# A four-layer graph kernel: Pool forms the fourth head's weights in every second unit of the last layer's later chunks, with a re-ordered end and earlier shifts in layer 0

## The chip, the cores and the metric

The kernel runs on one core of one Trainium2 chip. The metric is device time in microseconds (us), the median of several executions. The core's engines run side by side, each from its own queue of instructions, and wait for each other through semaphores: PE (TensorE, matrix products into the eight PSUM banks), DVE (VectorE), ACT (ScalarE), Pool (GpSimd) and SP, which only issues transfers here.

## The reference

The input is x (2708 nodes x 256 features) and a sparse matrix adj (2708 x 2708, non-negative, diagonal set). Four graph layers follow each other, each as x = layernorm(x + layer(x, adj)). Cut to the two that the change touches:

```python
# layer 0: three attention heads (and two GRU cells, left out here)
att = jnp.where(edge_adj > 0, e_plus[None, :], NEG_INF)
att = jax.nn.softmax(att, axis=1)
edge_support += att * edge_adj @ hW            # per head; adj without its diagonal
...
# layer 3: four heads of 64 features
h = (x @ W).reshape(n, HEADS, C)
e = leaky_relu(s_src[:, None, :] + s_dst[None, :, :], 0.2)
e = jnp.where((adj > 0.5)[:, :, None], e, -1e9)
alpha = softmax(e, axis=0)
out = jnp.einsum('ijh,ihc->jhc', alpha, h).reshape(n, 256) + bias
```

## The kernel before

The nodes are cut into T = 22 tiles of 128 rows; the last has 20. A sweep computes a result for all 2708 target columns, chunk by chunk; for each chunk it goes over the 22 source tiles. One tile in one chunk is a *unit*, and n = c x 22 + t numbers the units of a sweep. All loops over units are written out on every engine; the order of the code is the order in each engine's queue.

**The last layer (layer 3)** has CW = 3 chunks of 1,024, 1,024 and 660 columns, 66 units. The softmax's exponential is factored, so that a head's weight is a maximum of two known factors times the mask:

- SP loads a strip of adj (`strip3`, three buffers).
- ACT makes the mask from it in two passes (`above`, `masked`; L1493, L1500), bf16, three buffers. `masked(n)` waits until DVE has used unit n-3's mask.
- DVE forms the weights, one `scalar_tensor_tensor` a head, four a unit (L2116): PM3 = max(r3, s) x mask, f32, as wide as the chunk, three buffers. Unit n waits until PE is done with unit n-3.
- PE multiplies: features of heads 0 and 1 into banks 0 and 1, of heads 2 and 3 into banks 2 and 3 (L1164), and the sums of the weights, the degrees, into banks 4 and 5 (L1177), in matmuls that fill a quarter of the array's columns each. A unit of 1,024 columns is 32 + 16 recorded matmuls.

At a chunk's end ACT copies the six banks into rawT3 (`chunk_out`, three copies, L1508), when all matmuls of the chunk are done; PE opens each accumulator of the next chunk (L897) when its copy is there. The chunk's eight tiles of output are finished in pairs among the units of the next chunk (`pair_at`): PE turns a pair back (`backs`, six transposes, L1148), DVE makes the divisors (`divisors`, L2071 to L2077), Pool adds a term for rows without an edge (two tensor_tensor of 256 columns a tile, L833 and L835), ACT scales the eight head pieces (`scaled`, L1517), DVE adds (`added`, L2084) and takes statistics, ACT the root (L1524), DVE normalizes (`normed`, L2102), SP stores. The last chunk's three pairs (`LAST`) come one after another at the end. In layer 2 Pool has adds of 256 columns (L813) beside DVE weights of 496 (L2043).

**Layer 0's weighted sweep** has six chunks of 4, 4, 4, 3, 3 and 4 tiles (512, 512, 512, 384, 384 and 404 columns) and 132 units. Per unit: ACT `distances` (two relu passes, L1315), DVE `clamped` (L1752), ACT `exponentials` (L1322), DVE `weighted` (L1770), PE 12 recorded matmuls (L1051; 4 in the last unit, L1054). The weights E have three buffers; `distances(n)` and `clamped(n)` wait for PE to end unit n-3. The softmax's denominators of the later tiles come from work that goes on between the units: for each row tile a bias (L1677) and three heads, each one long custom DVE operation of 2708 columns (L1687), its negation (L1698) and a long ACT exponential (L1286). `ROWS_AT` says at which units these stand. When a chunk's rows are ready, its shifts are made: ACT a logarithm (`denominators`, L1292, with a table load before and one after it), DVE `shifts`, PE `maxima_turned`, ACT `maxima_out`, and SP stores a row (m_rows), waits for the store and spreads it to all partitions (m_bc), all in `maxima_row` at t = 20 of the chunk before. The first unit of the chunk waits for it.

Of the kernel before, what the change touches and what calls it, by code (L numbers as in the profile page):

```python
# [22 lines left out]
R = P  # L23
# [129 lines left out]
class WideLoad:  # L153


    def __init__(self, i):
# [17 lines left out]
SHIFTS_AT = 16  # L174
assert all(ROWS_AT[i][H0] < (chunk_of(i) - 1) * T + SHIFTS_AT for i in ROWS_AT)
# [4 lines left out]
def build(nc, x, adj, gat_W, gat_a, e_Wih, e_Whh, e_bih, e_bhh, n_Wih, n_Whh, n_bih, n_bhh,  # L180
# [15 lines left out]
    with ExitStack() as ctx:  # L196
# [99 lines left out]
        E = sb(3, H0, W)  # L296
        units_end = top[0]
# [119 lines left out]
        ln1_x = sem("ln1_x")  # L417
# [54 lines left out]
        LAST = range((CW - 1) * DT // 2, T // 2)  # L472

# [125 lines left out]
        def maxima_row(sp, c):  # L599
# [3 lines left out]
            load(sp, m_rows[c:c + 1, 0:H0 * nt * R].rearrange("a (k p) -> (a k) p", p=R), rows_s[0:H0 * nt, 0:R], m_out)  # L603
            sp.wait_ge(m_out, 16 * c)
# [36 lines left out]
        def _(sp):  # L641
# [58 lines left out]
            for n in range(3, UNITS):  # L700
# [4 lines left out]
                if c + 1 < CH and t == 20:  # L705
                    maxima_row(sp, c + 1)
# [29 lines left out]
            sp.wait_ge(ln2_x, T)  # L736
# [35 lines left out]
        def _(pool):  # L772
# [55 lines left out]
            for v in range(T // 2):  # L828
                pool.wait_ge(fin_zz, v + 1)
# [6 lines left out]
                pool.sem_inc(fin_zero, 1)  # L836


        def pe_project(pe, i, wcat, cols, between=None):
# [60 lines left out]
        def _(pe):  # L900
# [137 lines left out]
            for n in range(UNITS):  # L1038
# [9 lines left out]
                for h in range(H0 if t < T - 1 else 1):  # L1048
                    for f in range(KD):
                        if t < T - 1:  # L1050
                            ins = PE.matmul(bank(2 * (c % 2) + f)[:, 0:wid(c)], hs[0:R, m % 3, h * D + f * P:h * D + (f + 1) * P],  # L1051
                                            E[0:R, n % 3, h, 0:wid(c)], start=t == 0 and h == 0, stop=False)
                        else:
                            ins = PE.matmul(bank(2 * (c % 2) + f)[:, 0:wid(c)], hs_tail[0:STACK, f * P:(f + 1) * P],  # L1054
                                            E[0:STACK, n % 3, 0, 0:wid(c)], start=False, stop=True)
                ins.then_inc(s["mm_done"], 1)
                if t == 17 and c + 1 < CH:
                    maxima_turned(c + 1)
# [91 lines left out]
            for n in range(UNITS3):  # L1150
                c, t = divmod(n, T)
                halves = [(v, min(BANK, wide(c) - v * BANK)) for v in range(-(-wide(c) // BANK))]
                for h in range(0, H3, 2):
                    if t == 0:
                        if c:
                            pe.wait_ge(l3_read, RAW3 * (c - 1) + h // 2 + 1)
                        for v, w in halves:
                            opened(h + v)
                    if c == 0:
                        pe.wait_ge(l3_scaled, t + 1)  # L1160
                    pe.wait_ge(l3_p, n * H3 + h + 2)
                    for v, w in halves:
                        for q in range(P // DQ):
                            PE.matmul(bank(h + v)[q * DQ:(q + 1) * DQ, 0:w], proj3[0:kp(t), t, h * C3 + q * DQ:h * C3 + (q + 1) * DQ],  # L1164
                                      PM3[0:kp(t), n % 3, h + q * DQ // C3, v * BANK:v * BANK + w], start=False, stop=t == T - 1,
                                      skip_group_check=True)
                if t == 0:
# [5 lines left out]
                    for v, w in halves:  # L1173
                        opened(4 + v)
# [10 lines left out]
            for v in LAST:  # L1185
                backs(v)
# [966 lines left out]
```

## Time and profile before

| | |
|---|---|
| median of three runs | 2177.42 us (2175.49 to 2177.68) |
| the profiled execution | 2175.57 us |
| its span, first to last instruction | 2173.9 us |
| mean granted clock of PE | 0.977 of full |
| last layer's sweep, PE's first to last matmul | 1814.7 to 2150.5 |
| behind it, to the end of the span | 23.3 us |

The profile is one execution. Busy shares are shares of the span; matmuls are pipelined and their ends modelled, so that neighbouring ones overlap in the records, as DVE's do by under 0.1 us.

### The profile page before, as it was taken

The page shows a single profiled execution, that of the slowest core. Times are in us where ns is not written, and L with a number is a line of the kernel's source. Part 1 is how long each engine was busy: PE and PEld are TensorE (multiplying, and loading weights), DVE is VectorE, ACT ScalarE, POOL GpSimd, SP SyncE. Part 2 cuts the span into 40 slices and gives each one's busy share as a digit, 9 for nine tenths or more (in the row PEclk, how much of TensorE's full clock was granted, in tenths as well). Part 3 has the DMA queues.
Part 4 walks back from the last instruction along what each step waited for, and adds up shares of the span by engine and source line. Part 5 has one row for each costly group of instructions (what it writes and reads, how often), then busy time and mean ns, then how long its engine had stood idle before and what let it go on. Part 6 is the DMA issues. An engine that isn't in the chain of part 4 may idle for free.

```text
span 2173.9 us, 28504 instructions
## 1 busy us (share of the span) xinstructions
PE 2064.6 (95%) x10803; PEld 1159.6 (53%) x10803; DVE 1549.1 (71%) x2621; ACT 963.2 (44%) x1505; POOL 132.2 (6%) x169
## 2 busy tenths in 40 slices
PE   7999999899999999999999999999999978999996
PEld 4556665344444455555555534557999953333242
DVE  4665557797978875443778853444899956989997
ACT  3222226798888877664222210002121246644442
POOL 0000000000000000000001010000010040002011
PEclk9999999899999999999999999999999989999997
DMA  7665645455555554742000034541100115332231
GB/s 232 217 213 190 202 141 201 172 205 189 177 180 194 198 165 160 230 139 95 0 1 0 0 103 127 132 130 45 51 23 20 39 41 187 103 94 87 80 89 34
DMA packets 133176, 265.69 MB, mean 122 GB/s; under 512 B 15258, under 2 KB 62904, under 8 KB 130200
## 3 DMA queue, kind: packets, MB, share of 16 engines
q1 hardware_dynamic: 114712, 234.50, 34.0%
q10 hardware_dynamic: 18324, 29.34, 3.6%
q8 instruction: 86, 1.41, 0.3%
q14 instruction: 54, 0.44, 0.1%
HBM read 220.43 MB, written 43.36 MB: 121 GB/s over the span
## 4 chain that ended last, share of the span: by engine, by line
PE 64%; DVE 23%; ACT 8%; issue 4%; DMA 1%; POOL 0%; DVEq 0%; SPq 0%; ACTq 0%; POOLq 0%
PE banks L1051 20%; PE banks L954 9%; PE banks L1102 9%; PE banks L1136 6%; DVE arena L2116 5%; PE banks L1164 5%; PE banks L943 3%; DVE arena L2043 3%; PE banks L1177 3%; ACT arena L1286 2%; PE banks L995 2%; PE banks L861 2%; DVE arena L1687 2%; DVE arena L1770 1%; DVE arena L1871 1%
## 5 line engine op out<-in xcount | busy, mean ns | idle before, releaser
L1051 PE MATMUL banks<-arena 128*128 128x512 f32 (+2 forms) x1512 | 588.4, 548 | 19.4 <-DVE arena L1770 19.2
L1051 PEld LDWEIGHTS banks<-arena 128*128 128x128 f32 x1512 | 285.4, 191 | 312.2 <-issue 234.8
L1770 DVE TENSOR_TENSOR arena<-arena 128x1536 f32<-128x1536 f32 (+4 forms) x132 | 201.6, 1527 | 157.8 <-ACT arena L1322 150.4
L2116 DVE SCALAR_TENSOR_TENSOR arena<-arena 128x1024 f32<-128x1024 f32 (+3 forms) x264 | 293.1, 1181 | 16.0 <-PE banks L1177 13.2
L1164 PE MATMUL banks<-arena 128*32 128x512 f32 (+3 forms) x2112 | 221.3, 555 | 13.5 <-DVE arena L2116 13.5
L954 PE MATMUL banks<-arena 128*128 128x512 f32 (+4 forms) x528 | 222.5, 543 | 0.2 <-ACT arena L1227 0.2
L1136 PE MATMUL banks<-arena 128*124 128x129 f32 (+2 forms) x1936 | 217.7, 274 | 4.0 <-DVE arena L2043 3.3
L1136 PEld LDWEIGHTS banks<-arena 128*124 128x124 f32 (+2 forms) x1936 | 214.6, 186 | 7.3 <-DVE arena L2043 4.8
L1102 PE MATMUL banks<-arena 128*128 128x512 f32 (+4 forms) x528 | 207.7, 547 | 5.1 <-DVE arena L1872 3.7
L1315 ACT ACTIVATE arena<-arena 128x512 f32<-128x512 f32 (+4 forms) x264 | 162.8, 662 | 82.7 <-PE banks L1051 76.5
L1687 DVE CUSTOM_DVE_ANT_0 arena<-arena 128x2708 f32<-128x2708 bf16 (+1 forms) x66 | 196.2, 2973 | 1.6 <-DMA arena<-e_rows 1.3
L1322 ACT ACTIVATE arena<-arena 128x1536 f32<-128x1536 f32 (+4 forms) x132 | 170.7, 1294 | 40.1 <-DVE arena L1752 39.4
L2043 DVE SCALAR_TENSOR_TENSOR arena<-arena 128x496 f32<-128x496 f32 (+2 forms) x264 | 171.9, 709 | 21.1 <-PE banks L1136 14.4
L1286 ACT ACTIVATE arena<-arena 128x2708 f32<-128x2708 f32 (+1 forms) x66 | 168.0, 2546 | 11.7 <-DVE arena L1698 11.7
L1227 ACT COPY arena<-banks 128x512 f32<-128x512 f32 (+4 forms) x132 | 70.8, 536 | 210.3 <-PE banks L943 209.9
L1102 PEld LDWEIGHTS banks<-arena 128*128 128x128 f32 (+1 forms) x528 | 98.8, 190 | 105.1 <-issue 73.9
L1164 PEld LDWEIGHTS banks<-arena 128*32 128x32 f32 (+1 forms) x2112 | 70.9, 111 | 148.9 <-issue 128.6
L1635 DVE TENSOR_SCALAR arena<-arena 128x512 bf16<-128x512 f32 (+4 forms) x132 | 52.2, 395 | 112.9 <-ACT arena L1227 112.6
L1858 DVE TENSOR_SCALAR arena<-arena 128x512 uint8<-128x512 f32 (+4 forms) x132 | 51.9, 399 | 97.0 <-DMA arena<-adj_T 96.7
L954 PEld LDWEIGHTS banks<-arena 128*128 128x128 f32 (+1 forms) x528 | 89.6, 190 | 51.6 <-issue 36.1
L1177 PE MATMUL banks<-arena 128*32 128x512 f32 (+3 forms) x1056 | 114.6, 548 | 0.0
L1500 ACT ACTIVATE arena<-arena 128x1024 bf16<-128x1024 f32 (+1 forms) x66 | 69.1, 1047 | 65.5 <-DVE arena L2116 65.4
(224 smaller groups left out, 2236.4 us busy)
## 6 DMA issues: line engine op xcount, KB each, us to landing
arena<-hw_rows SPq DMA_DIRECT2D x126, 384.0 KB, 3.1
arena<-adj_T SPq DMA_DIRECT2D x126, 256.0 KB, 3.2
arena<-in_adj SPq DMA_DIRECT2D x17, 1354.0 KB
arena<-in_adj SPq DMA_DIRECT2D x42, 512.0 KB
adj_T<-arena ACTq DMA_DIRECT2D x63, 256.0 KB, 2.3
arena<-adj_T SPq DMA_DIRECT2D x84, 192.0 KB, 3.0
arena<-in_adj SPq DMA_DIRECT2D x15, 1024.0 KB
arena<-in_adj SPq DMA_DIRECT2D x15, 768.0 KB
```

Source lines behind the costliest of these rows:

```text
L954: PE.matmul(bank(2 * (c % 2) + f)[:, 0:w], xnat[0:k, t, f * P:(f + 1) * P], AT[0:k, n % 4, 0:w], start=t == 0, stop=t == T - 1)
L1051: ins = PE.matmul(bank(2 * (c % 2) + f)[:, 0:wid(c)], hs[0:R, m % 3, h * D + f * P:h * D + (f + 1) * P], E[0:R, n % 3, h, 0:wid(c)], start ...
L1102: ins = PE.matmul(bank(2 * (c % 2) + f)[:, 0:wid(c)], xd[0:kp(t), t, f * P:(f + 1) * P], strips1[0:kp(t), n % 4, 0:wid(c)], start=t == 0, ...
L1136: ins = PE.matmul(bank(b0 + k // 3)[0:nr, (k % 3) * (C2 + 1):(k % 3 + 1) * (C2 + 1)], PM2[0:kp(t), n % 3, h, r * R2:r * R2 + nr], proj2[0: ...
L1164: PE.matmul(bank(h + v)[q * DQ:(q + 1) * DQ, 0:w], proj3[0:kp(t), t, h * C3 + q * DQ:h * C3 + (q + 1) * DQ], PM3[0:kp(t), n % 3, h + q * D ...
L1177: ins = PE.matmul(bank(4 + v)[h * DQ:(h + 1) * DQ, 0:w], g3[0:kp(t), t, h, :], PM3[0:kp(t), n % 3, h, v * BANK:v * BANK + w], start=False, ...
L1286: S.activation(srow[0:kp(i), j % 2, :], srow[0:kp(i), j % 2, :], ACT.Exp, bias=negm[0:kp(i), h, i:i + 1], accum_out=den[0:kp(i), h, i:i + ...
L1322: S.activation(e, e, ACT.Exp, scale=-1.0).then_inc(s["y_ok"], 1)
L1687: link(V.tensor_tensor_reduce(out=srow[0:nr, sl, :], in0=bias[0:nr, :], in1=e_bc[0:nr, h, :], scale=1.0, scalar=3 * NEG, op0=ALU.add, op1= ...
L1770: V.tensor_tensor(e, e, a, ALU.mult).then_inc(s["p_ok"], 1)
L2043: V.scalar_tensor_tensor(PM2[0:k, n % 3, h, 0:w], r2_bc[0:k, h, c * CW2:c * CW2 + w], smalls[0:k, 4, h * T + t:h * T + t + 1], mask2[0:k, ...
L2116: V.scalar_tensor_tensor(PM3[0:k, n % 3, h, 0:w], r3_bc[0:k, h, c * WW:c * WW + w], smalls[0:k, 4, h * T + t:h * T + t + 1], mask3[0:k, n ...
```

## The change

Three things are changed together.

1. In the last layer, for every odd t of the second and third chunk but the very last unit (`by_pool`, 21 units), Pool forms head 3's weights in two instructions, a tensor_scalar (maximum) and a tensor_tensor (times the mask), with a semaphore of its own, l3_q; DVE forms three heads there. `weights_there` waits on both. Pool's terms for rows without an edge (`zero_terms`) are queued between these.
2. The last layer's end: `chunk_out` copies the banks of features as soon as their last matmul is done (l3_out). In the last unit PE does the degrees first, then the features of heads 0 and 1, the degrees' six transposes, the features of heads 2 and 3, and twelve transposes. DVE makes all divisors at once, and scales and adds in one instruction a head and tile, straight from PSUM; ACT's scalings and two of Pool's three rounds fall away there (their terms come to DVE).
3. In layer 0, the shifts of the chunks after the first two are made 2 to 10 units earlier (`SHIFTS_AT`), the store and the spread of the maxima stand a unit apart in SP's queue, rows 18 to 21 have other places (`ROWS_AT`), and the two chunks of 384 columns use the buffer of the weights as four parts (`E_narrow`, `weights_of`, `weights_free`). Two semaphores (ln1_x, ln2_x) become one.

```diff
-           14: (46, 47, 48, 49), 15: (50, 51, 52, 54), 16: (55, 56, 57, 58), 17: (59, 60, 61, 62), 18: (64, 65, 66, 67),
-           19: (69, 70, 72, 74), 20: (76, 77, 79, 81), 21: (83, 84, 86, 88)}
+           14: (46, 47, 48, 49), 15: (50, 51, 52, 54), 16: (55, 56, 57, 58), 17: (59, 60, 61, 62), 18: (64, 65, 67, 69),
+           19: (71, 72, 74, 76), 20: (78, 79, 81, 83), 21: (85, 86, 88, 90)}
...
-SHIFTS_AT = 16
+SHIFTS_AT = {0: 16, 1: 14 + T, 2: 12 + 2 * T, 3: 12 + 3 * T, 4: 6 + 4 * T}
+SHIFTS = {n: c + 1 for c, n in SHIFTS_AT.items()}
...
+        def by_pool(n):
+            return n >= T and n % T % 2 == 1 and n < UNITS3 - 1
...
+        def weights_there(eng, n, h):
+
+            eng.wait_ge(l3_p, vector_weights(n) + min(h + 1, H3 - by_pool(n)))
+            if h == H3 - 1 and pool_weights(n + 1):
+                eng.wait_ge(l3_q, pool_weights(n + 1))
...
+        def weights_of(n):
+            if n in NARROW:
+                return E_narrow[:, (n - NARROW[0]) % 4]
+            return E[:, (n if n < NARROW[0] else n - NARROW[-1] - 1) % 3]
+
+        def weights_free(eng, n):
+            if n >= 3:
+                eng.wait_ge(sw["C"]["mm_done"], n - 3 if n in NARROW[3:] else n - 2)
...
-                if c + 1 < CH and t == 20:
-                    maxima_row(sp, c + 1)
+                if n - 4 in SHIFTS:
+                    maxima_stored(sp, SHIFTS[n - 4])
+                if n - 5 in SHIFTS:
+                    maxima_spread(sp, SHIFTS[n - 5])
...
+            pool.wait_ge(rest_bc["r3"], 16)
+            for n in range(T, UNITS3):
+                c, t = divmod(n, T)
+                if by_pool(n):
+                    k, w = kp(t), wide(c)
+                    pool.wait_ge(l3_mm, n - 2)
+                    pool.wait_ge(l3_mask, n + 1)
+                    p = PM3[0:k, n % 3, H3 - 1, 0:w]
+                    link(G.tensor_scalar(p, r3_bc[0:k, H3 - 1, c * WW:c * WW + w],
+                                         smalls[0:k, 4, (H3 - 1) * T + t:(H3 - 1) * T + t + 1], None, ALU.max))
+                    G.tensor_tensor(p, p, mask3[0:k, n % 3, 0:w], ALU.mult).then_inc(l3_q, 1)
+                if pair_at(n, 5) is not None:
+                    zero_terms(pair_at(n, 5))
+            zero_terms(LAST[-1])
...
+            degrees(UNITS3 - 1).then_inc(l3_mm, 1)
+            features(UNITS3 - 1, 0)
+            pe.wait_ge(fin_scaled, LAST[0])
+            pe.wait_ge(l3_read, RAW3 * (CW - 1) + 1)
+            for i, g in enumerate(LAST_TILES):
+                ins = PE.transpose(bank(6, 2)[:, i * P:(i + 1) * P], rawT3[:, 2, g % DT * R:(g % DT + 1) * R], ident)
+            ins.then_inc(tail_ps, 1)
+            features(UNITS3 - 1, 2)
+            for k in range(RAW3 - 1):
+                pe.wait_ge(l3_read, RAW3 * (CW - 1) + k + 2)
+                for g in LAST_TILES:
+                    ins = PE.transpose(turned_back(g)[:, k * P:(k + 1) * P], rawT3[:, k, g % DT * R:(g % DT + 1) * R], ident)
+                    if k and g % 2:
+                        ins.then_inc(tail_ps, 1)
...
             def chunk_out(c):
-                act.wait_ge(l3_mm, (c + 1) * T)
                 if c:
                     act.wait_ge(back_ps, c * DT // 2)
-                for k in range(RAW3):
+                for k in (0, 1, 2) if c < CW - 1 else (2, 0, 1):
+                    if k < 2:
+                        act.wait_ge(l3_out, 2 * c + k + 1)
+                    else:
+                        act.wait_ge(l3_mm, (c + 1) * T)
                     S.copy(rawT3[:, k, 0:wide(c)], bank(2 * k, 2)[:, 0:wide(c)]).then_inc(l3_read, 1)
...
-                if c + 1 < CH and t == SHIFTS_AT + 1:
-                    shifts(c + 1)
+                if n - 1 in SHIFTS:
+                    shifts(SHIFTS[n - 1])
...
+            def last_terms(v, terms, factor):
+                for g in (2 * v, 2 * v + 1):
+                    nr = kp(g)
+                    for h in range(H3):
+                        f = slice(h * C3, (h + 1) * C3)
+                        x = xnat[0:nr, g, f]
+                        ins = V.scalar_tensor_tensor(x, terms(g)[0:nr, f], factor[0:nr, g, h:h + 1], x, ALU.mult, ALU.add)
+                link(ins)
...
-                for h in range(H3):
+                for h in range(H3 - by_pool(n)):
                     if n == 0:
                         dve.wait_ge(r3_first[h], 16)
...
-            divisors(LAST[0])
+            last_divisors()
+            for v in LAST[:-1]:
+                last_terms(v, lambda g: sum_bc, zz3)
             for v in LAST:
-                added(v)
-                if v + 1 in LAST:
-                    divisors(v + 1)
-                normed(v)
+                last_added(v)
+                if v > LAST[0]:
+                    normed(v - 1)
+            normed(LAST[-1])
```

## Rows read from the trace of the kernel before

**Rows 1.** The page's table of engines: busy us (share of the span), instructions.
```profile
PE 2064.6 (95%) x10803; PEld 1159.6 (53%) x10803; DVE 1549.1 (71%) x2621; ACT 963.2 (44%) x1505; POOL 132.2 (6%) x169
```

**Rows 2.** Timeline of PE, last layer: start us, us, engine, line, operation, tiles, count.
```profile
1884.83 3.66 PE L1164 MATMUL banks<-arena 128*32 128x512 f32 x32
1889.99 3.67 PE L1164 MATMUL banks<-arena 128*32 128x512 f32 x32
...
2084.32 2.40 PE L1164 MATMUL banks<-arena 128*32 128x512 f32 x32
2087.66 2.40 PE L1164 MATMUL banks<-arena 128*32 128x512 f32 x32
...
2091.91 1.32 PE L1164 MATMUL banks<-arena 128*32 128x512 f32 x16
```

**Rows 3.** Timeline of DVE, second chunk's units 3 and 4; in brackets idle time and its releaser.
```profile
1942.77 4.87 DVE L2116 SCALAR_TENSOR_TENSOR arena<-arena 128x1024 f32<-128x1024 f32 x4 [5.64 <-PE banks L1177]
1947.93 4.88 DVE L2116 SCALAR_TENSOR_TENSOR arena<-arena 128x1024 f32<-128x1024 f32 x4 [0.29 <-PE banks L1177]
```

**Rows 4.** DVE's groups by shape, 1959.8 to 2053.5 and 2066.9 to 2147.8: busy, mean ns, idle.
```profile
L2116 DVE SCALAR_TENSOR_TENSOR arena<-arena 128x1024 f32<-128x1024 f32 x60 | 76.3, 1341 | 0.0
...
L2116 DVE SCALAR_TENSOR_TENSOR arena<-arena 128x660 f32<-128x660 f32 x72 | 63.4, 950 | 2.8 <-PE banks L1177 2.8
```

**Rows 5.** PE's groups, 1942.6 to 2052.4 and 2066.7 to 2147.0: busy, mean ns, idle.
```profile
L1164 PE MATMUL banks<-arena 128*32 128x512 f32 x644 | 73.6, 593 | 2.0 <-DVE arena L2116 2.0
...
L1164 PE MATMUL banks<-arena 128*32 128x512 f32 (+1 forms) x643 | 51.0, 450 | 6.0 <-DVE arena L2116 6.0
```

**Rows 6.** Timelines of Pool and of DVE, the first pair's turn in the second chunk.
```profile
1959.64 0.62 POOL L833 TENSOR_TENSOR arena<-arena 128x256 f32<-128x256 f32 x1 [160.99 <-DVE arena L2074]
1960.34 1.50 POOL L835 TENSOR_TENSOR arena<-arena 128x256 f32<-128x256 f32 x1
1961.92 1.48 POOL L833 TENSOR_TENSOR arena<-arena 128x256 f32<-128x256 f32 x1
...
1961.26 4.79 DVE L2116 SCALAR_TENSOR_TENSOR arena<-arena 128x1024 f32<-128x1024 f32 x3
```

**Rows 7.** Timelines of DVE and of Pool in layer 2, the same microseconds.
```profile
1619.56 4.10 DVE L2043 SCALAR_TENSOR_TENSOR arena<-arena 128x496 f32<-128x496 f32 x4 [0.38 <-PE banks L1136]
...
1619.72 3.40 POOL L813 TENSOR_TENSOR arena<-arena 128x256 f32<-128x256 f32 x3
```

**Rows 8.** Pool's groups by shape, 0 to 25 us (two rows) and 1790 to 2150.
```profile
L769 POOL TENSOR_TENSOR arena<-arena 128x128 f32<-128x128 f32 x4 | 1.5, 414 | 14.3 <-DMA arena<-in_adj 14.3
L783 POOL MEMSET arena<- 128x704 f32 x1 | 0.7, 691 | 0.0
...
L822 POOL TENSOR_TENSOR arena<-arena 128x256 f32<-128x256 f32 x1 | 0.7, 727 | 0.4 <-PE banks L851 0.4
```

**Rows 9.** Chunk boundaries: a stretch (busy us, granted clock), PE's timeline, DVE's timeline.
```profile
1926.30:1933.30 7.00, 5.90 (x49) 1.36 (x48) 5.92 (x5) 1.05 (x2) 0.00 (x0) 0.83 0.00 0
...
1933.32 1.04 PE L897 MATMUL banks<-arena 128*128 128x512 bf16 x2 [1.12 <-ACT arena L1508]
...
2066.93 5.88 DVE L2116 SCALAR_TENSOR_TENSOR arena<-arena 128x660 f32<-128x660 f32 x7 [2.78 <-PE banks L1177]
```

**Rows 10.** The end: stretch with PE, PEld, DVE, ACT, Pool busy, then a DVE group.
```profile
2150.60:2173.90 23.30, 4.45 (x18) 3.02 (x18) 10.35 (x44) 7.50 (x30) 7.52 (x12) 0.55 0.09 30
...
L2084 DVE TENSOR_TENSOR arena<-arena 128x512 f32<-128x512 f32 (+2 forms) x4 | 2.1, 548 | 2.5 <-POOLq L836 2.5
```

**Rows 11.** Layer 0: stretch of the fourth chunk, chain that ended last, timelines of PE, ACT.
```profile
744.90:842.40 97.50, 87.19 (x259) 47.85 (x257) 69.69 (x78) 78.64 (x93) 6.83 (x3) 0.98 0.51 171
...
772.02 2.91 DVE arena L1687 x2
...
780.63 2.90 DVE arena L1687 x2
...
821.22 5.80 PE L1051 MATMUL banks<-arena 128*128 128x384 f32 x12 [2.75 <-DVE arena L1770]
...
625.74 1.34 ACT L1315 ACTIVATE arena<-arena 128x512 f32<-128x512 f32 x2 [1.63 <-DMA arena<-m_rows]
```

More of the change, by code:

```diff
@@ L173 @@
 LOAD_AT = {ROWS_AT[i][H0] + 1: i + 1 for i in range(RPC, T - 1)}
-SHIFTS_AT = 16
-assert all(ROWS_AT[i][H0] < (chunk_of(i) - 1) * T + SHIFTS_AT for i in ROWS_AT)
+SHIFTS_AT = {0: 16, 1: 14 + T, 2: 12 + 2 * T, 3: 12 + 3 * T, 4: 6 + 4 * T}
+assert all(ROWS_AT[i][H0] < SHIFTS_AT[chunk_of(i) - 1] for i in ROWS_AT)
+SHIFTS = {n: c + 1 for c, n in SHIFTS_AT.items()}
+NARROW = range(sum(s == RPC for s in SIZES[:CH - 1]) * T, (CH - 1) * T)
+assert all((SIZES[c] == RPC) == (c * T not in NARROW) for c in range(CH))
 ROWS_END = ROWS_AT[T - 1][H0]
@@ L827, in _, with zero_terms @@
             pool.wait_ge(sum_ok, 2)
-            for v in range(T // 2):
-                pool.wait_ge(fin_zz, v + 1)
+            def zero_terms(v):
+                pool.wait_ge(fin_zz, min(v, LAST[0]) + 1)
                 for nr, ts in pair_parts(v):
@@ L1149, in backs, with halves, features, degrees @@
                 ins.then_inc(back_ps, 1)
-            for n in range(UNITS3):
+            def halves(c):
+                return [(v, min(BANK, wide(c) - v * BANK)) for v in range(-(-wide(c) // BANK))]
+            def features(n, h):
                 c, t = divmod(n, T)
[L1152 to L1166, printed above, removed]
+                if t == 0:
+                    if c:
+                        pe.wait_ge(l3_read, RAW3 * (c - 1) + h // 2 + 1)
+                    for v, w in halves(c):
+                        opened(h + v)
+                if c == 0:
+                    pe.wait_ge(l3_scaled, t + 1)
+                weights_there(pe, n, h + 1)
+                for v, w in halves(c):
+                    for q in range(P // DQ):
+                        ins = PE.matmul(bank(h + v)[q * DQ:(q + 1) * DQ, 0:w], proj3[0:kp(t), t, h * C3 + q * DQ:h * C3 + (q + 1) * DQ],
+                                        PM3[0:kp(t), n % 3, h + q * DQ // C3, v * BANK:v * BANK + w], start=False, stop=t == T - 1,
+                                        skip_group_check=True)
+                if t == T - 1:
+                    ins.then_inc(l3_out, 1)
+            def degrees(n):
+                c, t = divmod(n, T)
                 if t == 0:
@@ L1178, in _ @@
                                         PM3[0:kp(t), n % 3, h, v * BANK:v * BANK + w], start=False, stop=t == T - 1, skip_group_check=True)
-                ins.then_inc(l3_mm, 1)
+                return ins
+            for n in range(UNITS3 - 1):
+                c, t = divmod(n, T)
+                features(n, 0)
+                features(n, 2)
+                degrees(n).then_inc(l3_mm, 1)
                 v = pair_at(n, 3)
@@ L1305, in distances @@
                     shifts_there(act, c)
-                if n >= 3 and not general:
-                    act.wait_ge(s["mm_done"], n - 2)
+                if not general:
+                    weights_free(act, n)
                 if n < 3:
```

88 lines of the change are left out of this document (55 added, 33 removed).

## The prediction

> **What bounds the kernel now.** I read the page first: Pool is busy 6% of the span [rows 1], which invites moving work to it. But the shares are means over stages, so I took the last layer by stretches. In its first chunk TensorE (PE) paces: its units start 5.16 us apart (1884.83, 1889.99), in the third chunk 3.34 us apart when fed (2084.32, 2087.66), and 0.91 more where a pair is turned back between them (2091.91) [rows 2]. DVE needs 4 x 1.20 = 4.79 us for a unit of 1,024 columns (four instructions in 4.88, less the 0.09 by which neighbours overlap) and waits 0.29 us before each [rows 3]. From the second chunk on DVE also finishes one pair of output tiles every four units, so that its 19 units from 1942.77 to 2053.5 take 110.7 us, 5.8 each, against PE's 5.16 + 0.91/4 = 5.4. DVE is then never idle: zero idle before the 60 weight instructions of 1959.8 to 2053.5 and 2.8 us before the 72 of the third chunk [rows 4]. Yet PE stands still little: 2.0 us of the second chunk's 110 and 6.0 of the third's 80 as separate gaps [rows 5]. By unit starts, 20 units at 5.16 and four turn-backs make 106.9 of 109.8, and 20 at 3.34 with four make 70.5 of 80.3. So a DVE that cost nothing would give 2.9 + 9.8 = 12.7 us at most.
>
> **The Pool part: what it takes from DVE.** By_pool is true for 11 units of the second chunk and 10 of the third. Each takes one weight instruction from DVE: 1.20 us at 1,024 columns, and (0.90 - 0.08) = 0.82 at 660.
>
> **What it gives back.** Pool gets two instructions per such unit, a tensor_scalar and a tensor_tensor as wide as the one removed. The trace shows what Pool and this very DVE instruction do to each other. Pool's 256-wide tensor_tensor takes 0.62 us alone and 1.48 to 1.50 beside DVE weights [rows 6]: it waits for the running one. DVE in turn makes three weights in 4.79 us instead of 2 x 1.20 + 1.28 = 3.68, though Pool did only one operation for each [rows 6]. One 256-wide Pool operation thus costs DVE some 0.38 us. In layer 2, beside three Pool adds, four 496-wide instructions take 4.10 [rows 7]; alone they would take 4 x 0.65 + 0.08 = 2.68 (0.65 from 0.82 at 660, less 164 columns at 1.04 ns, the slope between 1,024 and 660): 0.47 for an add. They take turns, they don't overlap. Being served in turn, DVE loses Pool's own time less about 0.25 (0.62 - 0.38).
>
> The Trainium skill says it of the chip ("SBUF — State Buffer", Who interferes with whom): a DVE instruction with two SBUF inputs and a GpSimd instruction that reads SBUF lock each other out for the whole instruction. By that rule DVE would lose the full 0.62, not 0.38; the sum below would be 9 us larger. The row decides for 0.38. The rule speaks against this change as a whole, and the trace agrees with that.
>
> Sizes. Tensor_tensor at 1,024: four times the 256-wide loss is 1.5 as the lower end; going on with the slope from 0.41 (128 wide) to 0.73 (256 wide) gives 2.6 alone, so 2.4 lost [rows 8]. I take 2.0, between them. The trace has no Pool tensor_scalar. It can't be quicker than a memset, which reads nothing: 0.69 at 704 [rows 8], so 1.0 at 1,024, 0.7 lost; nor slower than the two-input form, 2.0 lost. I take 1.1, near the memset since it has one input stream. Together 3.1 lost (2.2 to 4.4) against 1.2 saved: DVE is worse by 1.9 (1.0 to 3.2) per unit. At 660 the same lines give 1.95 (1.4 to 2.6) against 0.82: worse by 1.13 (0.6 to 1.8).
>
> **Where it lands.** Walk DVE from its last long wait, 1942.77 [rows 3], 1.1 us earlier because the gap before it goes (below). Unit 3: 3.6 + 3.1, unit 4: 4.8, unit 5: 6.7, divisors 0.8: 1960.7, where the profile has 1959.8, the start of the stretch in rows 4; +0.9. From there it has no slack: eight Pool units (7 to 21), 8 x 1.9 = 15.2, so +16.1. Third chunk: unit 1 adds 1.1, the wait of 2.78 before unit 3 [rows 9] is used up, leaving +14.4; nine more, 9 x 1.13 = 10.2: **+24.6 us** when DVE ends its last weight. Low ends: +10.8; high ends: +44. Pool isn't itself late: per four units it has two weights of about 6 us with their turns and four 256-wide operations of 1.5, 18 of 28 us. PE has to wait for whichever of the two ends last, and its slack in the second chunk is only 0.6 per unit. Pool runs ahead because the mask and the buffer of unit n are there once unit n-3 is done. The extra wait on PE's and ACT's queues costs nothing unless Pool is last.
>
> **Chunk boundary.** PE idles 1.12 us before the accumulators are opened, for ACT's copies [rows 9]. They now start when the first features of the last unit are done, about 4 us earlier, ahead of the gap: 1.1 gained at the first boundary (in the walk). At the second DVE sets the time, so nothing.
>
> **The tail.** From DVE's last weight (2147.8) to the end is 26.1 us, 23.3 of it behind PE's last matmul; in these DVE works 10.35 and the rest is waiting in turn on PE, on ACT's scalings and on Pool [rows 10]. Now, from the same point: degree sums and first features 1.1 each (a third of 3.34), six transposes 1.3 (0.91 in the flow), four small DVE steps 0.9: 4.4. Then 16 terms of 64 columns at 0.20 (0.82 at 660, less 596 columns at 1.04 ns) 3.2, and the last pair's four Pool operations beside them, 4 x 0.38 = 1.5: 9.1. The second features, ACT's two copies and twelve transposes hide there (without that cover they end at about 7.6, so nothing shows yet). Then 24 terms, 4.8; what is left of DVE's 10.35 without the additions (2.1, [rows 10]) and the three rounds of divisors (some 2.2), 6.1; hand-overs 0.8; store and end as now 2.3. Sum 23.1: **-3.0** (-1 to -6). What goes from the path is ACT's 24 scalings and Pool's turns; what comes on it is DVE's 40 small terms.
>
> **Layer 0.** Its fourth chunk (384 columns) isn't PE-bound: 97.5 us with PE busy 87.2 [rows 11]. The chain goes round DVE and ACT: row head 2.91, its negation, row exponential, unit exponential, weights, clamp, and the next head 8.61 us later (772.02, 780.63), for two units [rows 11]; PE would need 82.7 for the chunk if each of 21 units took 5.16 x 384/512 = 3.87. A fourth buffer doesn't shorten that ring: it frees waits on PE, and the first three narrow units keep the old one. I give it 0 to 1. The new places of the rows take one head of ten out of this chunk (about 1.5 us) and the logarithm, with two table loads, from right behind a row exponential: its stall of 2.75 before 821.22 [rows 11] halves. With the start of the chunk (rows' heads no longer on three units running) I get 4.0 (2 to 6). Earlier shifts also take away ACT's wait of 1.63 for the m_rows load at the second boundary [rows 11], of which a row exponential behind it hides most: 1.0 (0 to 2). Together **-5.0** (-2 to -8). The store and the spread of the maxima are now two steps of SP's queue, with one unit's loads between them; those are issued sooner than now. Loads ahead stay four deep.
>
> **Sum.** 24.6 - 3.0 - 5.0 = +16.6 on the profiled execution's 2175.57: 2192.2. The median of the runs is 1.85 us above that execution: 2194; I say 2193.
>
> **The rivals.**
> - *No turns to speak of* (Pool's two-step form interferes little, or Pool gets in where DVE waits). Then PE paces: 12.7 + 1.1 + 3.0 + 5.0 = 21.8 less: about 2155. Pool's and DVE's times beside each other speak against it [rows 6]. With x lost per weight at 1,024 (0.63 x at 660) the whole sum is about 14.3 x - 28.6: even at 2.0, faster by more than 0.2% under 1.7.
> - *Only the tensor_tensor interferes* (one input stream passes beside DVE). Loss 2.0 and 1.3: 8 x 0.8 + 0.5 - 2.8 + 9 x 0.48 = +8.4, less 8.0: 2178, no change. Nothing in the trace speaks to it directly.
> - *The clock goes too.* PE will now stand still 1 to 3 us in many units. Today the granted clock falls to the lower of its two levels (1.2 for 2.4 GHz) for part of 1926.3 to 1933.3, 0.83 on average, round the 1.12 us gap [rows 9]; the 12 matmuls behind the 2.75 us gap take 5.80 instead of 4.1 [rows 11]. At the lower level PE needs 10.3 us a unit and would itself pace. With this, or Pool prices at the high ends: about 2212.
>
> **How the numbers follow.** Turns as worked out 0.57, its own range 2178 to 2212; the clock or the high prices 0.13; one stream only 0.16; no turns 0.12; something else 0.02. What a measurement can tell from no change is 0.2%, 4.4 us. Faster: no turns, and a third of one stream: 0.18. Same: half of one stream and the low edge of the first case: 0.13. Slower: 0.69. Range 2170 to 2212, leaving out the no-turns case and half of the clock case.
>
> **What would show it.** DVE's weights beside Pool's: two operations of Pool each, 1.2 to 1.5 us longer than alone, and some DVE weight instructions of 2 to 3.5 us start to start. If these stay at 1.20, the whole forecast falls. The last layer's second chunk about 14 to 18 us longer, the third about 8 longer, PE with gaps before most odd units; first boundary without a gap; from DVE's last weight to the end 23; layer 0's fourth chunk 93 instead of 97.5. The prediction goes wrong first by Pool's tensor_scalar price, which is taken from a memset.

## The result, and the profile after

Before: 2177.18 us, after: 2181.91 us (medians of 16 runs each, 2172.72 to 2181.32 and 2179.48 to 2185.94); ratio 1.002, interval 1.0013 to 1.0028. The change makes the kernel slower by 4.7 us; 16 had been forecast. The profiled execution took 2180.24 us, span 2178.4, clock 0.981.

The page's engines, against [rows 1]:

```profile
PE 2064.0 (95%) x10803; PEld 1151.5 (53%) x10803; DVE 1568.8 (72%) x2625; ACT 957.4 (44%) x1481; POOL 222.3 (10%) x203
```

DVE has 21 weight instructions fewer and is busy 19.7 us longer; 5.6 of that lie in the new end (below), nearly all the rest in the weights' chunks. The groups of DVE and PE in the same stretches as [rows 4, 5] (second chunk 1954.0 to 2056.4 for DVE and 1942.6 to 2062.2 for PE, third 2070.4 to 2156.3 and 2070 to 2155.5), then Pool's from 1910 to 2156:

```profile
L2223 DVE SCALAR_TENSOR_TENSOR arena<-arena 128x1024 f32<-128x1024 f32 x53 | 83.4, 1639 | 0.0
L2173 DVE TENSOR_SCALAR arena<-arena 128x2 f32<-128x2 f32 x4 | 3.3, 827 | 0.1
...
L2223 DVE SCALAR_TENSOR_TENSOR arena<-arena 128x660 f32<-128x660 f32 x63 | 65.5, 1106 | 2.8 <-PE banks L1239 2.8
...
L1220 PE MATMUL banks<-arena 128*32 128x512 f32 x600 | 70.1, 595 | 10.1 <-DVE arena L2223 9.7
...
L1220 PE MATMUL banks<-arena 128*32 128x512 f32 x320 | 42.1, 598 | 11.5 <-DVE arena L2223 11.5
...
L886 POOL TENSOR_SCALAR arena<-arena 128x1024 f32<-128x1024 f32 x10 | 36.1, 3611 | 149.0 <-PE banks L1239 147.9 <-POOL arena L875 1.1
L886 POOL TENSOR_SCALAR arena<-arena 128x660 f32<-128x660 f32 x10 | 24.2, 2424 | 25.9 <-PE banks L1239 24.8 <-POOL arena L875 1.1
L888 POOL TENSOR_TENSOR arena<-arena 128x1024 f32<-128x1024 f32 x10 | 22.5, 2253 | 0.8
```

A DVE weight lasts 1639 ns in the mean for 1341 [rows 4], so seven instructions fewer (53 for 60) cost 7 us more. PE's idle time for DVE has grown from 2.0 to 9.7 and from 6.0 to 11.5 us. Pool waits for buffers that PE has to free and for its own work ahead, and PE never waits for Pool: Pool ended each weight 1.8 us or more before PE's features of heads 2 and 3 started.

How one weight of Pool costs DVE: Pool's timeline, then DVE's, read from three starts, each row covering two neighbouring instructions:

```profile
2035.06 3.53 POOL L886 TENSOR_SCALAR arena<-arena 128x1024 f32<-128x1024 f32 x1 [0.27 <-POOL arena L875]
2038.67 2.32 POOL L888 TENSOR_TENSOR arena<-arena 128x1024 f32<-128x1024 f32 x1
...
2034.22 3.71 DVE L2223 SCALAR_TENSOR_TENSOR arena<-arena 128x1024 f32<-128x1024 f32 x2
2035.80 3.33 DVE L2223 SCALAR_TENSOR_TENSOR arena<-arena 128x1024 f32<-128x1024 f32 x2
2037.85 4.21 DVE L2223 SCALAR_TENSOR_TENSOR arena<-arena 128x1024 f32<-128x1024 f32 x2
```

The weight that starts at 2035.80 ends at 2034.22 + 3.71 = 2037.93, and the next starts at 2037.85: 2.06 us from start to start instead of 1.20, so Pool's tensor_scalar costs 0.86, though it lasts 3.53 itself; the weight at 2037.85 inside that span takes its normal 1.28 (2035.80 + 3.33 = 2039.13). The one behind it ends at 2037.85 + 4.21 = 2042.06 after 3.02 us: the tensor_tensor costs 1.74. At 660 columns the same reading gives 0.55 and 1.10.

Not every weight meets DVE so. Pool's tensor_tensor of unit t = 17, with a DVE instruction of two elements a row out of the statistics of a finished pair, and the DVE instruction of the same kind in e9 (an experiment below), where Pool's tensor_scalar ran beside it:

```profile
2020.37 1.99 POOL L888 TENSOR_TENSOR arena<-arena 128x1024 f32<-128x1024 f32 x1
...
2021.35 1.04 DVE L2173 TENSOR_SCALAR arena<-arena 128x2 f32<-128x2 f32 x1
```

```profile
2009.41 4.26 POOL L886 TENSOR_SCALAR arena<-arena 128x1024 f32<-128x1024 f32 x1 [7.31 <-PE banks L1239]
...
2012.06 0.17 DVE L2173 TENSOR_SCALAR arena<-arena 128x2 f32<-128x2 f32 x1
2012.14 1.28 DVE L2223 SCALAR_TENSOR_TENSOR arena<-arena 128x1024 f32<-128x1024 f32 x1
```

In the first, the tensor_tensor costs DVE 0.87 (1.04 for 0.17) instead of 1.74; in the second the tensor_scalar costs nothing. In the kernel after, t = 13, 17 and 21 of the second chunk are such units.

The end, against [rows 10]: a stretch with the columns given there, then DVE's timeline.

```profile
2157.60:2178.43 20.83, 6.50 (x54) 3.83 (x46) 15.93 (x69) 2.74 (x6) 2.62 (x4) 0.56 0.14 46
```

```profile
2159.63 0.18 DVE L2180 COPY arena<-banks 128x24 f32<-128x24 f32 x1 [2.48 <-PE banks L1257]
...
2160.62 4.51 DVE L2193 SCALAR_TENSOR_TENSOR arena<-arena 128x64 f32<-128x64 f32 x16
2165.16 1.63 DVE L2193 SCALAR_TENSOR_TENSOR arena<-banks,arena 128x64 f32<-128x64 f32 x8
```

DVE is now the busy engine there (15.93 of 20.8 us, before 10.35 of 23.3), and from its last weight (2156.30) to the end it is 22.1 us instead of 26.0.

**Where the difference sits.** The last layer cut at six points that every trace has: PE's first matmul of the layer (1), DVE's start of unit 6 in the second chunk (2), its end of unit 21 (3), its start of unit 3 in the third chunk (4), the end of its last weight (5), the end of the span (6). In us:

| kernel | 1-2 | 2-3 | 3-4 | 4-5 | 5-6 |
|---|---|---|---|---|---|
| before | 145.2 | 93.7 | 13.4 | 80.9 | 26.0 |
| after | 144.8 | 102.2 | 14.0 | 85.9 | 22.1 |
| e1: merged parts, no Pool weights | 144.3 | 93.7 | 11.2 | 80.9 | 22.1 |
| e2: Pool part alone | 145.7 | 102.2 | 14.7 | 85.9 | 26.2 |
| e3: layer 0 part alone | 145.3 | 93.7 | 13.4 | 80.9 | 27.0 |
| e4: end part alone | 144.6 | 93.7 | 11.2 | 80.9 | 22.2 |
| e5: Pool writes constants | 144.2 | 85.4 | 18.4 | 75.2 | 22.1 |
| e6: tensor_scalar alone | 144.2 | 89.8 | 14.1 | 77.9 | 22.1 |
| e7: tensor_tensor alone | 144.6 | 94.5 | 14.1 | 80.4 | 22.1 |
| e8: second chunk alone | 145.0 | 102.2 | 12.4 | 80.9 | 22.1 |
| e9: t = 1, 5, 9, ... | 144.0 | 96.5 | 17.4 | 82.3 | 22.1 |
| e10: t = 3, 7, 11, ... | 144.4 | 99.2 | 12.9 | 84.2 | 22.1 |

(Two more executions with the old end, e3 and e11, have 27.0 in 5-6, so the old end itself varies by 1 us.)

After against before: -0.4, +8.5, +0.6, +5.0 and -3.9, with the layer's start 5.25 us earlier (1814.67, 1809.42): +4.6, the difference of the spans being 4.5.

### The profile page after: what moved, and what is told of

Its sections match the earlier page's. It is cut to its first block, busy times and chain, and to the rows that moved or that the text cites. A ratio compares the mean times of both kernels' runs of the same rounds, so it can differ in the third digit from the quotient of the medians.

```text
span 2178.4 us, 28619 instructions
## 1 busy us (share of the span) xinstructions
PE 2064.0 (95%) x10803; PEld 1151.5 (53%) x10803; DVE 1568.8 (72%) x2625; ACT 957.4 (44%) x1481; POOL 222.3 (10%) x203
## 4 chain that ended last, share of the span: by engine, by line
PE 64%; DVE 24%; ACT 6%; issue 3%; DMA 1%; SPq 0%; DVEq 0%; POOL 0%; ACTq 0%; POOLq 0%
PE banks L1106 20%; PE banks L1009 9%; PE banks L1157 9%; PE banks L1191 6%; DVE arena L2223 6%; PE banks L1220 5%; PE banks L998 3%; DVE arena L2120 3%; PE banks L1239 3%; PE banks L1050 2%; DVE arena L1766 2%; ACT arena L1365 2%; PE banks L916 2%; DVE arena L1948 1%; DVE arena L1847 1%
## 5 line engine op out<-in xcount | busy, mean ns | idle before, releaser
L2223 DVE SCALAR_TENSOR_TENSOR arena<-arena 128x1024 f32<-128x1024 f32 (+3 forms) x243 | 301.1, 1309 | 15.5 <-PE banks L1239 12.7
L1220 PEld LDWEIGHTS banks<-arena 128*32 128x32 f32 (+1 forms) x2112 | 65.7, 111 | 171.0 <-issue 125.1
```

What stands on the lines that cost most here:

```text
L1220: ins = PE.matmul(bank(h + v)[q * DQ:(q + 1) * DQ, 0:w], proj3[0:kp(t), t, h * C3 + q * DQ:h * C3 + (q + 1) * DQ], PM3[0:kp(t), n % 3, h + ...
L2223: V.scalar_tensor_tensor(PM3[0:k, n % 3, h, 0:w], r3_bc[0:k, h, c * WW:c * WW + w], smalls[0:k, 4, h * T + t:h * T + t + 1], mask3[0:k, n ...
```

## The experiments

Ratios are to the kernel before, run on the same chip beside each.

**Which part costs what: e1 to e4.** e1 is the kernel after with `by_pool` always false.

```diff
-            return n >= T and n % T % 2 == 1 and n < UNITS3 - 1
+            return False
```

e2 is the kernel before with `by_pool`, its waits and Pool's loop alone; e3 the kernel before with the layer 0 edits alone; e4 the kernel before with the new `chunk_out` and the new end of the last layer alone. Where an expectation speaks of 17 weights, these are the ones inside stretches 2-3 and 4-5; each of these kernels moves all 21.

> The two merged parts alone, with every weight of the last layer on VectorE. Theory A (the merged parts gain what the comparison of the traces shows, about 5.2 us before the last layer and 4.0 us behind its last weight; the Pool part alone loses): 9 us under the kernel before, about 2168 us, VectorE's last weight near 2142.6 us. Theory B (the gains and the loss depend on each other: with the last layer starting 5 us earlier, or without Pool's work, VectorE waits for something else): less than half of that, about 2173 us or more.

> The Pool part alone on the kernel before. Theory A (17 weights by Pool cost VectorE a net 8.5 us in the second chunk and 5.0 us in the third): 13 to 14 us slower, about 2191 us, with the same prices per pair of instructions: beside Pool's tensor_scalar one 1,024-wide weight of VectorE takes 2.06 us from start to start, beside its tensor_tensor 2.9 us. Theory B (part of the loss comes from how the merged parts shift the tail or the opening against Pool): 8 us or less. The prediction on record would have 24.6 us here.

> The first layer's part alone. Theory A: what the sweep of layer 0 wins, about 5.2 us at the last layer's first matmul, arrives at the end in full, since the last layer's order is unchanged: about 2172 us. Theory B (a later layer's clock halving or a wait gives it back): 2174 to 2177 us.

> The part on the last layer's end alone (chunks' ends, divisors, outputs). Theory A: the stretch from VectorE's last weight to the end falls from 26.1 to about 22.1 us and nothing else changes: about 2173 us. Theory B (the shorter end in the comparison came from Pool's or VectorE's load in the last units and not from this part): within 1 us of the kernel before.

| run | median us | ratio (interval) | difference |
|---|---|---|---|
| e1 | 2165.97 | 0.995 (0.9938 to 0.9963) | -11.0 |
| e2 | 2192.84 | 1.0071 (1.0058 to 1.0084) | +15.9 |
| e3 | 2169.84 | 0.997 (0.9959 to 0.9981) | -7.1 |
| e4 | 2170.49 | 0.9967 (0.9954 to 0.998) | -6.5 |

Theory A holds in kind: the parts add up. The Pool part costs 15.9 us on the kernel before, and 4.7 + 11.0 = 15.7 on top of e1. The merged parts win more than I read from two traces (11.0, not 9), and separately 13.6; their intervals (e1 8.1 to 13.5, e3 4.1 to 8.9, e4 4.4 to 10.0) allow both.

e4's 6.5 is seen in the table: 0.6 at the first boundary, 2.2 at the second, 3.9 at the end. "Nothing else changes", as theory A had it, is wrong by the 2.2. Two things make them up. PE's gap of 1.12 us ahead of the accumulators is there at the second boundary of before as well, and e4 has none. And PE's clock is at its lower level for less time. The stretch 2055 to 2070 (the granted clock is the third figure from the right), before, e4, after:

```profile
2055.00:2070.00 15.00, 13.88 (x130) 4.04 (x126) 12.22 (x16) 8.21 (x10) 0.00 (x0) 0.77 0.39 109
2055.00:2070.00 15.00, 15.00 (x134) 4.04 (x130) 14.37 (x19) 8.68 (x11) 0.00 (x0) 0.89 0.42 109
2055.00:2070.00 15.00, 15.00 (x114) 3.49 (x110) 12.81 (x16) 8.92 (x11) 3.85 (x2) 0.77 0.38 106
```

A clock of 0.77 over 15 us is some 6.9 us at half speed, 0.89 some 3.3; the difference is worth about 1.8 us to a busy PE. In before the gap lies within the spell, so the two don't add up in full. e1 and e8 have 0.89 round this boundary too, e2 0.77. So in the kernel after the Pool part takes the 2.2 back: by the delay of PE described under e8, and by the longer spell. That the new `chunk_out` or Pool's work sets the spell's length isn't shown.

**What Pool's instructions do to DVE: e5 to e7.** Each is the kernel after with another body for Pool's weight. e5 leaves the maximum and the mask of these weights out, e6 the mask, e7 the maximum.

```diff
 # e5
-link(G.tensor_scalar(p, r3_bc[...], smalls[...], None, ALU.max))
-G.tensor_tensor(p, p, mask3[0:k, n % 3, 0:w], ALU.mult).then_inc(l3_q, 1)
+link(G.memset(p, 1.0))
+G.memset(p, 1.0).then_inc(l3_q, 1)
 # e6
+G.tensor_scalar(p, r3_bc[...], smalls[...], None, ALU.max).then_inc(l3_q, 1)
 # e7
+G.tensor_tensor(p, r3_bc[...], mask3[0:k, n % 3, 0:w], ALU.mult).then_inc(l3_q, 1)
```

> The kernel after, but Pool writes the constant 1.0 twice where it would form a weight (the maximum and the mask of those 17 weights are left out). It tells the work taken off VectorE from what Pool's reads do to it. Theory A (VectorE is lengthened by instructions of Pool that read SBUF, and keeps its own time beside a write of a constant): VectorE's 1,024-wide weights stay at 1.20 us, 17 of them are gone, TensorE paces the units and the kernel ends near 2156 us. Theory B (any instruction of Pool takes turns with VectorE): a memset of 1,024 lasts 0.69 us alone, so VectorE loses up to 1.4 us a weight, and the time is 2168 us or more, no better than without Pool's work.

> The kernel after with Pool's tensor_scalar alone; the multiplication by the mask is left out for those 17 weights. Theory A (each such instruction costs VectorE 0.86 us at 1,024 and 0.55 us at 660 against 1.20 and 0.82 us saved): VectorE comes out ahead by 0.3 us a weight, so 4 to 5 us faster than with no weight on Pool, about 2163 us. Theory B (the tensor_scalar with a scalar from memory is what costs, and the tensor_tensor rides along): slower than without Pool's work, 2172 us or more.

> The kernel after with Pool's tensor_tensor alone (rows of r times the mask; the maximum is left out for those 17 weights). Theory A (1.74 us lost at 1,024 and 1.10 us at 660 against 1.20 and 0.82 us saved, less what falls beside VectorE's waits): 3 to 7 us slower than without Pool's work, about 2173 us. Theory B (the second read operand makes no difference; two instructions of one kind cost the same): like the kernel with the tensor_scalar alone, within 1.5 us of it.

| run | median us | ratio (interval) | difference | stretches 2 to 5, against e1 |
|---|---|---|---|---|
| e5 | 2159.8 | 0.9919 (0.9899 to 0.9938) | -17.8 | -6.9 |
| e6 | 2160.37 | 0.9923 (0.9902 to 0.9944) | -17.3 | -4.0 |
| e7 | 2169.33 | 0.9962 (0.995 to 0.9975) | -8.3 | +3.2 |

e1 has -11.0, so e5 and e6 are 6.8 and 6.3 us under it and e7 2.7 above. e7's profiled execution is the fastest of its ten (2161.32, its last layer starts at 1803.9), so its stretches are compared and not its span. Pool's and DVE's timelines, first of e5, then of e6, then of e7:

```profile
2018.67 0.95 POOL L886 MEMSET arena<- 128x1024 f32 x1 [8.35 <-PE banks L1238]
2019.68 0.95 POOL L887 MEMSET arena<- 128x1024 f32 x1
...
2015.98 7.27 DVE L2222 SCALAR_TENSOR_TENSOR arena<-arena 128x1024 f32<-128x1024 f32 x6
```

```profile
2013.24 2.84 POOL L886 TENSOR_SCALAR arena<-arena 128x1024 f32<-128x1024 f32 x1 [5.54 <-PE banks L1238]
...
2013.53 0.84 DVE L2172 TENSOR_SCALAR arena<-arena 128x2 f32<-128x2 f32 x1
2014.28 6.06 DVE L2222 SCALAR_TENSOR_TENSOR arena<-arena 128x1024 f32<-128x1024 f32 x5
```

```profile
1999.86 2.70 POOL L886 TENSOR_TENSOR arena<-arena 128x1024 f32<-128x1024 f32 x1 [0.24 <-POOL arena L875]
...
1997.42 11.01 DVE L2221 SCALAR_TENSOR_TENSOR arena<-arena 128x1024 f32<-128x1024 f32 x7
```

In e5 six weights beside two memsets take 7.27 us, 6 x 1.20 + 0.08: nothing lost, though Pool writes the same buffer. In e7 seven take 11.01 where 7 x 1.20 + 0.08 = 8.48 would do: 1.74 for this tensor_tensor, the rest for the 256-wide ones ahead of it. In e6 the tensor_scalar at 2013.24 falls on DVE's statistics and costs DVE 0.67 in a two-element instruction (0.84 for 0.17), and the five weights behind it take 6.06, none longer than alone, while it still runs. Theory A holds in all three: of these three bodies, the two that read cost DVE time and the one that only writes doesn't, and the two kinds that read have two prices. (e5's expectation took the 0.69 us of a memset of 704 columns for one of 1,024; that one lasts 0.95.)

The Trainium skill ("SBUF — State Buffer", Who interferes with whom) has this distinction: a DVE instruction with two SBUF inputs contends with a GpSimd one that reads SBUF, not with one that only writes. By that e5 had to be free, and the trace agrees (1.20 us a weight). Where contention does hold, it speaks of an exclusive lock, and spells that out as "for the whole instruction" under DVE's two-port modes; the prediction read it so for this pair as well. Of the tensor_tensor's 1.99 us at the shortest DVE loses 1.74, of the tensor_scalar's 2.84 only 0.86, so for this pair the measurement decides against the whole span.

In the table the stretches 2-3 and 4-5 hold 8 and 9 weights of Pool. Against e1, 8 x 1.20 = 9.6 us of DVE's work are saved in the first: e6 is 3.9 shorter, so a tensor_scalar costs (9.6 - 3.9)/8 = 0.71 in the mean, e7 0.8 longer, 1.3 for a tensor_tensor; both together 8.5 longer, 2.27. In the third chunk, with 7.4 saved: 0.49, 0.76 and 1.37. e6's body alone wins against e1 and e7's alone loses; but only both together make a weight.

**Where Pool's work falls: e8 to e10.**

```diff
-            return n >= T and n % T % 2 == 1 and n < UNITS3 - 1
+            return T <= n < 2 * T and n % 2 == 1                   # e8
+            return n >= T and n % T % 4 == 1 and n < UNITS3 - 1    # e9
+            return n >= T and n % T % 4 == 3 and n < UNITS3 - 1    # e10
```

> The kernel after with Pool's weights in the second chunk alone (11 units); the third chunk's are VectorE's again. Theory A (losses of the two chunks add up, each from its own pairs of instructions): of the 15.9 us that Pool's part costs, the second chunk keeps what the comparison with the kernel without Pool's work shows from the second chunk's first to the third chunk's first matmul, 10.6 us, so about 2176 to 2177 us. Theory B (the 3 us wait of VectorE ahead of the third chunk takes the second chunk's delay up, as the prediction on record has it): some 3 us less, 2173 us.

> The kernel after with Pool's weights only in units t = 1, 5, 9, 13, 17, 21 of the second chunk and 1, 5, 9, 13, 17 of the third (11 weights), where in the kernel after one of Pool's two instructions mostly runs beside VectorE's short instructions of the pair's end. Theory A (the loss depends on what VectorE runs beside Pool: a unit of this kind loses about 0.5 us net, 0 where VectorE waits): 3 to 5 us above the kernel without Pool's work, about 2170 us. Theory B (each weight costs the same, 15.9 us / 21 = 0.76 us): 8.3 us, 2174 us.

> The complement: Pool's weights only in units t = 3, 7, 11, 15, 19 of both chunks (10 weights), where both of Pool's instructions run beside VectorE's weights. Theory A: 0.86 + 1.74 - 1.20 = 1.4 us net each in four units of the second chunk, 0.55 + 1.10 - 0.82 = 0.83 us in four or five of the third: 9 to 11 us above the kernel without Pool's work, about 2176 us. Theory B (each weight costs the same): 7.6 us, 2173.6 us, and no more than the other ten or eleven.

| run | median us | ratio (interval) | above e1 |
|---|---|---|---|
| e8 | 2175.17 | 0.9993 (0.9982 to 1.0004) | 9.2 |
| e9 | 2171.59 | 0.9981 (0.9969 to 0.9993) | 5.6 |
| e10 | 2176.35 | 0.9996 (0.9982 to 1.001) | 10.4 |

e8: the second chunk's loss isn't taken up by the wait ahead of the third; 3-4 is 12.4, not less than e1's 11.2. The 1.2 us more are PE's: it starts the chunk's last unit 1.14 us before DVE's last weight of the chunk ends in e1, and 0.05 us after it in e8, as in e2 against before (there 3-4 grows by 1.25). The third chunk costs the other part. e9 and e10 in the chunks: four weights at t = 9, 13, 17, 21 cost 2.9 us together, four at t = 7, 11, 15, 19 cost 5.5, 1.4 each as the two prices say (0.86 + 1.74 - 1.20); in the third chunk 1.3 and 3.3. Sums 8.4 and 4.7, the kernel after has 8.5 and 5.0. So DVE's loss depends on what Pool's instruction meets: theory A. In e9's second chunk the unit t = 9 pays both prices in full; at t = 13, 17 and 21 the tensor_scalar runs beside the statistics and costs nothing, the tensor_tensor its 1.74. But this isn't the whole of e9's time: between points 3 and 4 its profiled execution has 17.4 us. PE's timeline of e9 there, then a stretch with the granted clock (third figure from the right):

```profile
2038.96 1.93 PE L1220 MATMUL banks<-arena 128*32 128x512 f32 x16 [0.25 <-DVE arena L2223]
2043.09 2.80 PE L1220 MATMUL banks<-arena 128*32 128x512 f32 x16 [2.20 <-DVE arena L2223]
...
2048.36 4.67 PE L1220 MATMUL banks<-arena 20*32 20x512 f32 x32
2052.79 3.65 PE L1239 MATMUL banks<-arena 20*32 20x512 f32 x16
```

```profile
2050.00:2060.00 10.00, 10.00 (x55) 2.16 (x48) 8.11 (x8) 5.54 (x7) 3.15 (x2) 0.54 0.09 31
```

Behind a gap of 2.20 us, and in the unit of 20 rows, the clock is at the lower of its two levels (1.2 for 2.4 GHz) for nearly the whole boundary; in e1 the same 32 and 16 matmuls take 3.64 and 1.90. In this execution stretches 2 to 5 are 10.4 us longer than e1's, 6.2 of them here, and the whole 6.4, since its last layer started 3.7 us earlier (1806.1, 1809.8). e9's runs spread from 2169.1 to 2181.7; how often the clock does this in them isn't known, so its median says less about DVE than the stretches do.

**Layer 0: e11 and e12,** one execution each (2178.67 and 2176.96 us, one of before beside them 2185.34: too few to compare; the stretches are read). e11 has only the four-part buffer (`E_narrow`, `weights_of`, `weights_free`) in the kernel before, e12 only the new `ROWS_AT`.

```diff
# e12
-           ... 18: (64, 65, 66, 67), 19: (69, 70, 72, 74), 20: (76, 77, 79, 81), 21: (83, 84, 86, 88)}
+           ... 18: (64, 65, 67, 69), 19: (71, 72, 74, 76), 20: (78, 79, 81, 83), 21: (85, 86, 88, 90)}
```

> The kernel before with one edit of layer 0: the weights' buffer as four parts in the two chunks of 384 columns. Stretches of the weighted sweep by TensorE's unit starts (fourth chunk 97.4 us in three of the traces with the old layer 0, 94.3 in all six with the new; fifth 84.3 and 84.9). Theory A (the ring over VectorE and ScalarE sets the fourth chunk, a fourth buffer doesn't shorten it): 97.4 and 84.3, unchanged within 0.5. Theory B (the buffer is what wins the 3.2 us): 94.3.

> The kernel before with one edit of layer 0: the new places of the rows 18 to 21. Theory A (one row head of about 3 us less in the fourth chunk, half of it on the path): the fourth chunk 1.5 to 2 us shorter, the fifth up to 1 us longer, the second's 112.8 us unchanged; what is left of the 3.2 us and the 1.9 us at the second boundary comes from the earlier shifts. Theory B (the rows' places alone win the fourth chunk's 3.2 us, the logarithm's place nothing).

The fourth and the fifth chunk, from PE's first matmul to the next chunk's: the kernel after, e11, e12.

```profile
740.96:835.23 94.27, 85.59 (x259) 46.98 (x257) 67.68 (x75) 75.96 (x91) 3.57 (x3) 1.00 0.55 176
835.23:920.16 84.93, 84.87 (x257) 49.09 (x258) 42.84 (x52) 56.49 (x75) 0.00 (x0) 0.98 0.64 204
```

```profile
747.72:845.12 97.40, 87.18 (x258) 47.85 (x257) 69.64 (x78) 78.46 (x93) 6.65 (x3) 0.98 0.52 170
845.12:929.22 84.10, 83.17 (x258) 48.44 (x258) 39.87 (x49) 54.09 (x73) 0.00 (x0) 1.00 0.63 206
```

```profile
745.62:841.22 95.60, 85.47 (x259) 46.95 (x257) 67.69 (x75) 76.22 (x91) 3.70 (x3) 1.00 0.53 174
841.22:926.73 85.51, 83.66 (x257) 47.90 (x258) 43.16 (x52) 57.60 (x75) 0.00 (x0) 1.00 0.64 205
```

Before has 97.44 and 84.31. The buffer does nothing. The rows' places win 1.8 us and give 1.2 back in the next chunk, into which one head moved (52 DVE instructions for 49). The other 1.3 of the fourth chunk go to what is left of the edit, the earlier shifts, by difference, which no run has alone; so do 2.0 us in the second chunk (112.9 before, 110.9 after). The last layer's first matmul wanders between executions of the same layer 0 (1814.7, 1816.5, 1819.8), so the sweep's own length is compared: three with the old layer 0 have 612.7, 610.3 and 613.3 us, the nine with the new 605.4 to 608.3: 5.7 less in the mean. Up to 1.7 of it is a spell of the lower clock at the second boundary (granted 0.83 from 630 to 640), which three of five traces with the old shifts have and none of the nine with the new; and e4's 613.3 hold a longer such spell in the fourth chunk (99.4 us).

## Why the prediction was wrong in size

The direction and most mechanisms held: Pool's reads delay DVE, PE waits for DVE, the merged parts are too small to pay for it. The forecast of +16.6 was 12 us too high: the walk of DVE to its last weight by 10.9 (24.6 against 13.7 in the kernel after), the tail by 0.9, the start of the last layer by 0.2. Its steps:

- *"Together 3.1 lost against 1.2 saved", "DVE is worse by 1.9".* **This is the first step that failed, a size.** Measured 0.86 and 1.74, together 2.60, net 1.4; at 660 columns 1.65, net 0.83, not 1.13. That is 4.0 us too much in the second chunk and 2.7 in the third. The tensor_tensor was drawn too long from the slope of two narrow instructions (it lasts 1.99 at the shortest, so "Pool's own time less about 0.25" is right for it); the tensor_scalar's 1.1 was a guess from a memset, near by luck: its bound "nor slower than the two-input form" is wrong for the duration (2.84 us at the shortest against 1.99), and duration and price have little to do with each other.
- *"From there it has no slack: eight Pool units, 8 x 1.9".* DVE is never idle, but it isn't always in an instruction that Pool hinders at the full price. This is the second step that failed: it prices every Pool unit alike. In the kernel after, five of the eight pay 2.60 and three (t = 13, 17, 21) 0.86 + 0.87, where the tensor_tensor meets the statistics of a finished pair: 18.2 in all less 9.6 saved is 8.6, and 8.5 is measured. e9 and e10 show it too: 0.7 against 1.4 a weight. Another 2.7 us too much in the second chunk and 2.5 in the third; there the same reading explains 1.8, the rest is open.
- *"The wait of 2.78 before unit 3 is used up."* Wrong, by about 3 us the other way: 3-4 grew by 1.25 in e2 where -1.7 was forecast. DVE waits there for PE to get over the boundary, and PE reaches the boundary 1.2 us later against DVE because DVE's weights were late. A wait for an engine that one has delayed oneself moves along; it is no slack.
- Together 24.6 - 4.0 - 2.7 - 2.7 - 2.5 + 2.9 - 0.4 (the stretch 1-2) = 15.2 for the Pool part; e2's four stretches have 15.3, its runs 15.9.
- *"At the second (boundary) DVE sets the time, so nothing"*: e4 wins 2.2 there, the gap and a shorter spell of the lower clock (above). The first boundary's 1.1 came as forecast: from PE's first matmul of the first chunk to that of the second 119.6 us in before, 118.5 in e4. The tail: 3.0 forecast, 3.9 measured; the time it named to the first terms, 4.4, is 4.3, and the 16 terms with Pool beside them 4.5 for 4.7.
- *Layer 0, -5.0*: -5.7 by the traces, -7.1 by e3's runs. Fourth chunk 3.2 less 0.6 given back in the fifth, not 4.0; boundary 2.0, not 1.0; and the clock spell. The buffer's "0 to 1" is 0.
- Rivals: "no turns" is what e5 is, and its time came within 5 us of the 2155 named for it; "only the tensor_tensor interferes" is refuted by e6's timeline, though the result fell near its time; of "the clock goes too", e9 shows the mechanism, and the kernel after has little of it (mean granted clock 0.981, before 0.977).

The runs point to e1, the merged parts without Pool's weights, as the version that beats both: 0.5% under before, some 16 us under after.

## What to carry to other kernels

Idle time of Pool is no free capacity beside a DVE that runs two-input instructions: price a move by how much later DVE's neighbour starts, not by Pool's own duration, and against what it takes off DVE. In this kernel one tensor_scalar of Pool for one DVE weight was a gain (e6), one tensor_tensor a loss (e7), and the two that a weight takes cost 2.3 to 2.6 us for 1.2 saved. Ask also what DVE does at that moment: beside the short statistics the same Pool instructions cost less. And when several changes are measured as one, run each alone: a gain of 11 us stood behind a total of +4.7.

## What the runs showed of the hardware

- Beside DVE's weights, a Pool tensor_scalar over 1,024 f32 columns (scalar from SBUF) lasts 2.84 to 4.96 us by the traces and holds one weight up by 0.86; a tensor_tensor lasts 1.99 to 2.91 and holds it up by 1.74; a memset lasts 0.95 and costs nothing. At 660 columns 0.55 and 1.10.
- A DVE tensor_scalar of two elements takes up to 1.05 us beside Pool's reads (0.17 alone), while the statistics instructions beside it keep their 0.43. In e9's second chunk it kept its 0.17 beside Pool's tensor_scalar three times.
- The granted clock falls to the lower of its two levels at both chunk boundaries of the last layer in every trace, also without a gap of PE: in the kernel after, PE is never idle between 1917 and 1945 us, and its 16 degree matmuls of 20 rows still take 3.05 us for 1.90. That the 1.12 us gap of [rows 9] caused the spell isn't borne out; what does isn't settled by these runs.
